# Fused attention and mixture-of-experts block: score passes of a head pair in a row, value block last in the step, causal mask of the maxima on VectorE

## The reference, cut to what matters

```python
scores = jnp.einsum('bhqd,bhkd->bhqk', q, k) * scale
causal_mask = jnp.triu(jnp.ones((Tx, Tx), dtype=bool), 1)
scores = jnp.where(causal_mask, -jnp.inf, scores)
attn = jax.nn.softmax(scores, axis=-1)
out = jnp.einsum('bhqk,bhkd->bhqd', attn, v)
...
x = x + ga * attention(h)
...
x = x + gb * experts(h2)
```

## Time and profile before

| | us |
|---|---|
| median of 3 runs | 3058.89 (3057.62 to 3067.77) |
| span of the profiled execution | 3061.1 |
| TensorE matmul busy | 2843.4 (93%) |
| VectorE busy | 2242.9 (73%) |
| ScalarE busy | 1779.3 (58%) |
| GpSimd busy | 1253.7 (41%) |

### The profile page before, as it was taken

The page is one execution under the profiler, slowest core; times in us unless marked ns, Lnnn a source line. Parts: engine busy times, 40 slices in busy tenths (PEclk is TensorE's granted clock), DMA queues, the critical chain, the costliest instruction groups (busy, mean ns, idle before and its releaser), DMA issues.

```text
span 3061.1 us, 61038 instructions
## 1 busy us (share of the span) xinstructions
PE 2843.4 (93%) x22500; PEld 1573.9 (51%) x22500; DVE 2242.9 (73%) x5047; ACT 1779.3 (58%) x2736; POOL 1253.7 (41%) x1557
## 2 busy tenths in 40 slices
PE   7888799999999999989999999987999999999997
PEld 4433333333433334433333333323888999999997
DVE  7888788888888888899998888822393225566477
ACT  2422466666566665656665566665556666666533
POOL 6766311213521114521114765554305753443176
PEclk9999899999999999999999999998999999999998
DMA  4854323313312322412323535245336765665486
GB/s 163 209 142 106 110 56 65 66 42 76 101 39 56 66 63 59 109 43 37 66 63 91 141 94 123 89 129 152 117 93 204 233 202 175 187 183 173 136 238 193
DMA packets 290690, 359.05 MB, mean 117 GB/s; under 512 B 65404, under 2 KB 243212, under 8 KB 290140
## 3 DMA queue, kind: packets, MB, share of 16 engines
q1 hardware_dynamic: 259516, 279.94, 33.8%
q0 software_dynamic: 26112, 71.34, 7.7%
q10 hardware_dynamic: 4768, 3.88, 0.5%
HBM read 206.25 MB, written 139.21 MB: 113 GB/s over the span
## 4 chain that ended last, share of the span: by engine, by line
PE 49%; ACT 13%; DVE 10%; POOL 7%; issue 7%; DMA 2%; ACTq 1%; POOLq 0%; SPq 0%; DVEq 0%
ACT P L1643 13%; PE PB L1165 10%; PE PB L1092 8%; PE PB L1181 7%; DVE mx L1460 6%; PE PB L1062 6%; PE PB L1039 6%; PE PB L1075 5%; POOL x_slots L1846 4%; PE PB L1106 2%; PE PB L1150 2%; ACTq L1652 1%; POOL yg L1859 1%; PE PB L1129 1%; POOL x_slots L1838 1%
## 5 line engine op out<-in xcount | busy, mean ns | idle before, releaser
L1460 DVE TENSOR_REDUCE mx<-PB 128x1 f32<-128x512 f32 (+3 forms) x2560 | 1406.9, 603 | 214.6 <-PE PB L1039 135.6
L1643 ACT ACTIVATE P<-PB 128x1024 f32<-128x1024 f32 (+3 forms) x1280 | 1095.4, 894 | 643.3 <-PE PB L1075 629.3
L1039 PE MATMUL PB<-KO,QO 64*128 64x512 bf16 (+3 forms) x2560 | 762.0, 353 | 61.5 <-DVE mx L1460 51.5
L1092 PE MATMUL PB<-P,V 128*17 128x512 f32 (+3 forms) x5120 | 599.2, 540 | 11.8 <-POOL P L1797 11.7
L1062 PE MATMUL PB<-QO,KO 64*128 64x512 bf16 (+3 forms) x2560 | 546.8, 353 | 60.0 <-ACT P L1643 33.0
L1039 PEld LDWEIGHTS PB<-KO,QO 64*128 64x128 bf16 x2560 | 203.5, 94 | 718.0 <-DVE mx L1460 533.0
L1075 PE MATMUL PB<-QO,KO 34*128 34x512 bf16 (+3 forms) x2560 | 520.0, 351 | 0.6 <-DMA QO<-nh 0.4
L1797 POOL TENSOR_SCALAR_AFFINE_SELECT P<-P 128x256 f32<-128x256 f32 x512 | 208.6, 414 | 678.8 <-ACT P L1643 673.1
L1165 PE MATMUL PB<-xT,ws 128*128 128x128 f32 x3432 | 433.7, 277 | 7.1 <-ACT xT L1726 7.0
L1165 PEld LDWEIGHTS PB<-xT,ws 128*128 128x128 f32 x3432 | 408.2, 193 | 9.7 <-ACT xT L1726 9.7
L1571 DVE TENSOR_TENSOR haT<-sl,PB 64x128 f32<-64x128 f32 x350 | 101.4, 290 | 411.8 <-ACT sl L1735 407.3
(11 more groups left out here) (178 smaller groups left out, 3218.7 us busy)
## 6 DMA issues: line engine op xcount, KB each, us to landing
xq<-x_slots SPq DMA_DIRECT2D x286, 128.0 KB, 2.8
qk_parts<-pt SPq DMA_DIRECT2D x192, 128.0 KB, 2.4
KO<-qk_parts SPq DMA_DIRECT2D x192, 128.0 KB, 4.1
y_slots<-yo SPq DMA_DIRECT2D x191, 128.0 KB
QO<-qk_parts SPq DMA_DIRECT2D x64, 256.0 KB, 3.4
rden<-rden_rows SPq DMA_DIRECT2D x256, 64.0 KB
y_slots<-mx SPq DMA_DIRECT2D x95, 128.0 KB
v_rows<-vst SPq DMA_DIRECT2D x16, 544.0 KB, 4.0
```

Of the source, the lines that this page charges most:

```text
L1039: mm = pe.matmul(PB[:, bank, 0:n], QO[half, k3, j, 128 * t:128 * t + 128], KO[half, k3, j, 512 * kc:512 * kc + n], start=True, stop=True)
L1092: mm = pe.matmul(PB[32 * j:32 * j + 17, 7, c0:512], V[:, g % 2, kt, 17 * j:17 * j + 17], P[:, pbuf(g, i, j // 2), j % 2, 0:n], start=kt == ...
L1460: dve.tensor_reduce(mx[:, j, t, kc:kc + 1], PB[:, u.bank[item], 0:n], AX.X, ALU.max).then_inc(s["mx"], 1)
L1643: act.activation(P[:, pbuf(g, i, p), :, 0:n], PB[:, 2 * p:2 * p + 2, 0:n], ACT.Exp, scale=0.25).then_inc(s["exp"], 1)
```

## The change

Three things change. The order of a step in `plan()`: `sa` of heads 3 and 2 come first, with one maximum between them, and their `sb` directly behind; then the same for heads 1 and 0 of the next step, with the maxima put between; the value block and the pumped items come last. The two masking products of a diagonal block go away. In their place VectorE reduces that block with `tensor_tensor_reduce`, which adds a mask (`mk`, bfloat16, in SBUF), writes the sum back to the PSUM bank and gives the maximum.

```diff
@@ plan()
-        if len(pend) == 2:
-            values(*pend.pop(0))
+        o("sa", g, i, 3)
         maxima(at + (quota + 2) // 4)
-        o("sa", g, i, 3)
         o("sa", g, i, 2)
-        maxima(at + quota // 2)
-        if ahead:
-            o("sa", *ahead, 0)
-            o("sa", *ahead, 1)
         o("sb", g, i, 3)
         o("sb", g, i, 2)
         o("exp", g, i, 1)
-        if i >= 2:
-            pumped(pumps)
+        maxima(at + quota // 2)
+        if ahead:
+            o("sa", *ahead, 1)
+        if ahead:
+            o("sa", *ahead, 0)
+        if ahead:
+            o("sb", *ahead, 1)
         maxima(at + quota // 2 + (quota + 2) // 4)
         if ahead:
             o("sb", *ahead, 0)
-            o("sb", *ahead, 1)
-        maxima(at + quota)
         if ahead:
             o("exp", *ahead, 0)
+        maxima(at + quota)
+        if len(pend) == 2:
+            values(*pend.pop(0))
+        if i >= 2:
+            pumped(pumps)
         send_rows()
@@ TensorE, max
-                    if kc == t // 4:
-                        pe.matmul(PB[:, bank, n - 128:n], pick[half, 0, :], tri[half, 0, :], start=False, stop=True, skip_group_check=True)
-                        mm = pe.matmul(PB[:, bank, n - 64:n], pick[half, 1, :], tri[half, 1, 64:128], start=False, stop=True,
-                                       skip_group_check=True)
@@ VectorE, max
-                    dve.tensor_reduce(mx[:, j, t, kc:kc + 1], PB[:, u.bank[item], 0:n], AX.X, ALU.max).then_inc(s["mx"], 1)
+                    if kc == t // 4:
+                        dve.tensor_tensor_reduce(PB[:, u.bank[item], 0:n], PB[:, u.bank[item], 0:n], mk[:, 512 - n:512], 1.0, -3.0e38,
+                                                 ALU.add, ALU.max, mx[:, j, t, kc:kc + 1]).then_inc(s["mx"], 1)
+                    else:
+                        dve.tensor_reduce(mx[:, j, t, kc:kc + 1], PB[:, u.bank[item], 0:n], AX.X, ALU.max).then_inc(s["mx"], 1)
```

More of the change, by code:

```diff
@@ L482, in program @@
         ident = A("ident", [128, 128], F32)
-        pick = A("pick", [128, 2, 128], BF16)
-        tri = A("tri", [128, 2, 128], BF16)
+        mk = A("mk", [128, 512], BF16)
         mhalf = A("mhalf", [128, 4], F32)
@@ L1196, in _ @@
             dve.memset(mhalf[:, :], -0.5).then_inc(s["c_k"], 1)
[L1197 to L1204, removed]
+            dve.memset(mk[:, 0:384], 0.0).then_inc(s["c_k"], 1)
+            dve.tensor_copy(mk[:, 384:512], cons[:, 1, :]).then_inc(s["c_k"], 1)
+            q.wait_ge(s["c_k"], 5)
             step = [0]
```

## The result

The changed kernel takes 3230.27 us (median of 4 runs, 3219.35 to 3245.57), the kernel before 3061.72 (median of 4). The ratio is 1.0555, with a 95% interval of 1.053 to 1.058: slower, as forecast, but by about 169 us where 78 were forecast, and outside the range of 3080 to 3215.

A forecast was written before the change was run, and what follows sets the result against it. It took attention steps to be held by engines waiting on each other, then TensorE as its own bound in the new order. 3061 + 123 + 8 - 8 - 45 = 3139, less 2, gave 3137 us; range 3080 to 3215.

The forecast's parts named there:

- What bounds the kernel now: Attention steps: engines wait on each other; group 15's wide step of 2.67 us is held through ScalarE, idle 0.73.
- the ring of ScalarE and TensorE: Attention step: `sa` waits for the second exponential, `sb` stands behind `sa`, and ScalarE waits for `sb`; TensorE idles 0.53 us.
- The new order, wide and mean step: TensorE's queue in attention: 3.06 us a wide step against 2.67, 2.71 in the mean; lean groups +8.2, +123 us in all.
- the waits of `sb`: Sign on TensorE: weight loads of `sb` waiting for `sa` in most steps, hundreds of us.
- waits of `sa` for ScalarE: Sign on TensorE: these waits, 185 us before the change, were to be nearly gone.
- The 2 us a group for the row DMAs: ScalarE issues eight row DMAs a head group; 1 us taken for each row of four, bounds 0 and 4 a group.
- Halves strictly in order: Rival on TensorE: matmuls on a free half cannot pass waiting ones; 114 us more, some 3245; chance 0.07.
- The term of 8 us: Diagonal blocks on VectorE: the dearer masked reduction delays maxima, +8 us, bounds 0 and 35.
- the rival in which VectorE becomes the bound: Attention steps: the new reduction costs over 0.4 us more, giving 3200 to 3320 us; chance 0.09.
- The other groups, -45 us: Groups above the lean pace: a third of their 134 us extra, partly waits, comes back; -45 us, bounds 0 and -67.
- The range: Whole kernel: 3080 to 3215 us, reaching past the forecast's own 3085 to 3185 for an expensive mask.
- the 8 us of credit: Group 15, without maxima: wide step 2.44 us against 2.67, taken as -8 us, bounds 0 and -15.

The follow-up runs named there:

- e8: e7 with the diagonal masks on VectorE in place of the masking products; 3067.45 us, ratio 1.003 to the kernel before.
- e7: Kernel before, `sb` of heads 3 and 2 ahead of the waiting `sa`, three maxima between, value block last, masks by products; 3084.54 us, ratio 1.0078.
- e3: Changed kernel with a step's first maximum behind both `sa` of heads 3 and 2 instead of between them; 3148.47 us, ratio 1.0288.
- e4: e3 with also the second maximum moved behind both `sa` of heads 1 and 0; 3092.09 us, ratio 1.0108.
- e6: Changed kernel with the plain reduction for diagonal blocks too, leaving out the causal mask of the maxima; 3228.26 us, ratio 1.0543.
- e12: Changed kernel without half of the attention output projection and half of the gate logits; 3206.89 us, ratio 1.0457.
- e5: Changed kernel with the pumped items (projection, routing, scatters) back behind the step's first exponential; 3246.14 us, ratio 1.0606.
- e2: Kernel before with the changed kernel's step order, masks still by the two products; 3272.9 us, ratio 1.0687.
- e1: Changed kernel with the step order of the kernel before, masks on VectorE; 3053.57 us, ratio 0.9971.
- e9: Kernel before's step order, masks on VectorE, value block at the step's end; another chip, 3221.76 us, ratio 0.9954.
- e11: e8 with the pumped items behind the first exponential; another chip, 3242.51 us, ratio 1.0019.

## Why the prediction was right and wrong

*What bounds the kernel now.* Right for group 15: the ring of ScalarE and TensorE. Taking it apart brings that group's wide steps from 2.67 to 2.45 us (e8), and to 2.48 in the changed kernel (2.44 forecast). For the groups with maxima it is not shown: e7 and e8 have no ring, and their lean groups take 102.9 and 100.6 us for the 102.3 and 100.9 of the old order.

*The new order, wide and mean step.* Right, and it is nearly the whole result: the starts agree within 0.02 us, the widest step is 3.10 us for 3.06, the lean group is 111.7 for 110.5, the waits of `sb` are the ones foretold, and e3 and e4 show the cause by moving one maximum. The term was +123 and measured +141. Of the signs, one did not come: waits of `sa` for ScalarE were to be nearly gone. The 2 us a group for the row DMAs no run tests.

*Halves strictly in order* fell: 997.49 before 997.71, above, as before the change (1005.65 before 1005.71). That the median of 3230 lies near that rival's 3245 is chance, since its lean group would have been 118.

*VectorE.* The term of 8 us measured next to none (e6: 0.1 us a lean group), and the rival in which VectorE becomes the bound fell. Each diagonal block was put at up to 0.21 more; between e6 and the changed kernel it is 0.04.

*The other groups, -45 us.* This is the step that failed, with the words "I take a third back". Measured, these groups are 15 us more over the lean pace than before, not 45 less: a miss of 60. What I had read as waits for banks and VectorE is in groups 3 and 4 TensorE's own work, 1.88 us a tile: 30 of the 31.3 us before and of the 34.5 after. e12, without half of the products, shows that nearly all of it is paid (8.7 of 10.4 us came off). The rows were there to count it from, and I had taken a share without counting. Six groups with projections held 118 of the 134 us, so little was there to give back. Of the 15 us that were added, 6 are in groups 3, 4 and 7, at a clock of 1.00, and 6 in group 9, at 0.92.

*The range.* Its upper end did not follow from the terms. With the credits of the other groups and of group 15 at 0 and the mask at 35 the sum is 3217, and with 4 us a group for the row DMAs 3247; I had stopped at 3185 and 3215.

*The clock.* No step of the prediction had it. Group 9 takes 123.8 us at a granted clock of 0.92; before, it took 108.5 at 1.00. That is 15.3 more, where a lean group takes 9.4 more and group 10, at 1.00 both times, 8.3 (117.6 for 109.3). Elsewhere the fall is in group 10: in e5 group 9 takes 115.1 us at 1.00 and group 10 123.0 at 0.93, in e2 120.3 at 1.00 and 127.6 at 0.93. So the fall costs such a group some 6 to 8 us, and it is not tied to one of the two. Group 15 stays at 104.3 for 104.2 although its wide steps are faster. Its first 17.5 us run at a granted clock of 0.52, and the 86.8 behind them at 1.00; the first stretch:

```profile
2178.70:2196.20 17.50, 16.92 (x81) 2.74 (x80) 0.51 (x2) 9.25 (x12) 5.99 (x8) 0.52 0.21 64
```

But the kernel before had a low stretch in that group too, 0.61 in its first 4.2 us: its mean was 0.94 and is 0.92 now. By an estimate from these two shares the difference is worth 2 us; where the rest of the 8 us of credit went is open.

The four timed runs of the changed kernel go with the clock: 3219.35 at 0.973, 3228.19 at 0.970, 3232.34 at 0.967, 3245.57 at 0.964. The profiled one, on which the terms stand, is the fastest, 11 below the median. The kernel before had 0.976 to 0.981 in its runs beside e1. What makes the clock fall more often in the new order no run separates.

The ledger for the miss of 93 us: 60 from the other groups, 18 less 8 from the lean groups and VectorE, 8 from group 15, 11 between the profiled run and the median. Another 4 are in how the forecast went from a span to a time: it took 2 off, and the time of a run is 1.8 above its span (3219.35 for 3217.6).

## What to carry to other kernels

Two matmuls that depend on each other by a semaphore want other work between them: here 0.44 us lie between their starts at 512 columns, and each independent matmul put there was worth 56 to 82 us over 600 steps. A ring found where a part of the work is missing (group 15) need not be what holds the rest. Before a wait is broken out of a ring, follow the one queue that is to be the new bound start by start, with the same durations; that gave the wide step within 0.05 us. The sum of the recorded waits doesn't give the loss: in e3 those of `sb` for `sa` fell from 525.5 us to 514.3, and the time by 82. And what a stage costs over a leaner one is to be counted in instructions of the engine that will be the bound before any of it is credited as waiting.

## What the hardware showed that was not expected

A reduction with a mask added costs VectorE almost nothing more than a plain one (0.04 us a block, e6): its accumulator read (140 ns as recorded) starts together with the next block's sum (both at 1030.07). A matmul on a free half starts ahead of an earlier one whose half is busy, before the change (1005.65 before 1005.71) and after it (997.49 before 997.71). On the chip of e9 to e11 the stage of the experts was longer, 1115.7, 1087.4 and 1102.2 us where the kernel before had 936.6 on another, while the attention took the same (e9's lean group 101.1 us, e1's 100.9); the window of e9's:

```profile
2114.70:3230.40 1115.70, 951.64 (x6413) 864.69 (x6414) 494.82 (x1466) 533.09 (x1210) 421.82 (x452) 0.93 0.49 151
```

TensorE does the same work there (951.64 us busy against 886, at a granted clock of 0.93 against 0.98) and stands still for 164 us against 51; what for is open.
